# A fused cross-attention and FFN kernel: the next context's parts made earlier, one transpose in another PSUM bank, two copies behind the last exponential

## The reference, cut to what matters

```python
x = x + xattn(layernorm(x), ctx, ctx, wq, wk, wv, wo_w, wo_b)
x = x + ffn(layernorm(x), W_in, b_in, W_out, b_out)
# xattn: q, k rotated (rope), v plain; 16 heads of 32 features; band |q - k| <= 128;
#        softmax(q k^T * sqrt(32)) v, then wo_w and wo_b
# ffn: weights rounded to 8 bits, activations to 16 bits, exact gelu between the products
```

## Time and profile before

| | |
|---|---|
| time before, median of 3 runs | 1230.52 us (1228.41 to 1232.91) |
| profiled execution, its own time | 1230.85 us |
| its span, first to last instruction | 1228.3 us |
| PE busy / DVE busy | 1148.1 us / 979.9 us |
| ACT busy / POOL busy | 639.9 us / 361.2 us |

### The profile page before, as it was taken

How to read it: one execution, slowest core, us unless ns; L and a number is a source line. 1 busy time by engine, 2 the same in 40 slices (tenths; PEclk the granted TensorE clock), 3 DMA queues, 4 the chain that set the end, 5 groups by cost and what they waited for, 6 DMA issues and landing times.

```text
span 1228.3 us, 23590 instructions
## 1 busy us (share of the span) xinstructions
PE 1148.1 (93%) x7884; PEld 767.8 (63%) x7928; DVE 979.9 (80%) x2541; ACT 639.9 (52%) x1001; POOL 361.2 (29%) x540
## 2 busy tenths in 40 slices
PE   6989999999999999999999867999999999999998
PEld 6857776877776777787677545444444444444443
DVE  6868989989899998998998746666666678777776
ACT  5254354345335435434533433655556568777774
POOL 1135336345444534634644331000000012111111
PEclk9989999999999999999999969999999999999999
DMA  8554664565565466456555532455554211667772
GB/s 269 127 135 109 170 175 118 152 176 138 142 177 149 110 173 165 113 164 171 146 139 145 143 121 77 144 204 199 204 206 175 95 60 35 187 219 239 237 223 94
DMA packets 100522, 191.10 MB, mean 156 GB/s; under 512 B 13376, under 2 KB 30912, under 8 KB 100416
## 3 DMA queue, kind: packets, MB, share of 16 engines
q1 hardware_dynamic: 100416, 189.75, 52.4%
HBM read 89.16 MB, written 43.91 MB: 108 GB/s over the span
## 4 chain that ended last, share of the span: by engine, by line
DVE 37%; PE 35%; issue 24%; DMA 2%; ACT 1%; SPq 1%; POOL 0%; DVEq 0%; POOLq 0%
PE bank L858 18%; DVE bank L1192 7%; PE bank L521 4%; PE bank L522 4%; PE bank L523 4%; DVE bn L1138 3%; DVE roped L1218 3%; DVE rt L1215 2%; DVE rt L1216 2%; DVE row_max L1192 2%; PE bank L605 2%; DVE neg_max L1233 2%; DVE x_res L1185 2%; DVE nt_t L292 2%; DVE nt_t L291 1%
## 5 line engine op out<-in xcount | busy, mean ns | idle before, releaser
L1192 DVE CUSTOM_DVE_ANT_0 bank<-bank,mask 128x256 f32<-128x256 f32 x512 | 201.8, 454 | 43.5 <-PE bank L605 36.6
L858 PE MATMUL bank<-wout_int,g_lo 128*128 128x512 bf16 x512 | 193.6, 379 | 1.1
L819 PE MATMUL bank<-qT_lo,win_int 128*128 128x512 bf16 x496 | 188.0, 379 | 1.2
L858 PE MATMUL bank<-wout_int,g_hi 128*128 128x512 bf16 x491 | 185.8, 379 | 0.3 <-issue 0.2
L819 PE MATMUL bank<-qT_hi,win_int 128*128 128x512 bf16 x474 | 179.6, 379 | 0.0
L961 ACT ACTIVATE probs<-bank 128x512 f32<-128x512 f32 x256 | 143.2, 604 | 36.8 <-PE bank L639 32.2
L1529 POOL TENSOR_SCALAR_AFFINE_SELECT probs<-probs 128x256 f32<-128x256 f32 x256 | 108.6, 427 | 80.4 <-ACT probs L961 74.3
L605 PE MATMUL bank<-k_st,q_st 96*128 96x256 f32 x512 | 98.8, 305 | 25.1 <-DVE row_max L1192 23.3
L1484 DVE TENSOR_TENSOR g_lo<-h_int,g_hi 128x512 f16<-128x512 f32 x128 | 89.1, 696 | 41.4 <-ACT g_hi L1101 37.8
L1522 POOL TENSOR_TENSOR x_res<-x_res,wo_b 128x512 f32<-128x512 f32 x32 | 43.4, 1375 | 253.8 <-DMA x_res<-in_x 246.5
L1069 ACT ACTIVATE h_ring<-bank,b_in,g_scale 128x512 f32<-128x512 f32 x96 | 73.0, 778 | 71.3 <-PE bank L819 54.8
(11 more groups left out here) (170 smaller groups left out, 2725.5 us busy)
## 6 DMA issues: line engine op xcount, KB each, us to landing
hidden_scratch<-h_ring SPq DMA_DIRECT2D x96, 256.0 KB, 2.1
h_ring<-hidden_scratch SPq DMA_DIRECT2D x96, 256.0 KB, 2.8
k_st<-k_hi SPq DMA_DIRECT2D x128, 128.0 KB, 2.7
q_st<-q_hi SPq DMA_DIRECT2D x128, 128.0 KB, 2.6
xq<-x_scratch SPq DMA_DIRECT2D x16, 1024.0 KB, 5.9
x_ln<-in_x SPq DMA_DIRECT2D x16, 512.0 KB, 4.5
ctx_raw<-in_ctxT SPq DMA_DIRECT2D x16, 512.0 KB, 5.0
k_st<-k_lo SPq DMA_DIRECT2D x64, 128.0 KB, 2.7
```

Source lines behind the costliest of these rows:

```text
L819: mm = pe.matmul(bank[f % 4][:], win_int[:, c, f * P:(f + 1) * P], part[:, par, c], start=c == 0 and part is qT_hi, stop=c == KC - 1 and p ...
L858: return pe.matmul(bank[4 * par + u][:], part[:, f % 4, u * P:(u + 1) * P], wout_int[:, f], start=f == 0 and part is g_hi, stop=f == FC - ...
L1192: dve.tensor_tensor_reduce(sc, sc, mask[:, (1 - qb) * P:(1 - qb) * P + S], 1.0, NEG, ALU.add, ALU.max, row_max[:, qb, n:n + 1]).then_inc(m ...
```

## The change

Four things move, and nothing is computed differently. (1) Transpose 1 of x goes to bank 6 instead of bank 5. It then waits for `oT_out` (bank 6 copied out in the step before) instead of `den_done`; V tile 0, which writes bank 6 next, waits for `xt_lo`; Q half 1, which writes bank 5, waits for `den_done`. (2) ScalarE's `ctx_hi(b+2)` moves from behind exponential 9 to the front of `max_copy`. (3) GpSimd's four `ctx_lo(b+2)` move from behind bands 10 to 13: two in front of band 0, one behind band 1, one behind band 3. (4) ScalarE's `oT_copy(b, 0)` and `centre(b-1, 0)` move from behind exponentials 12 and 13 to behind the last.

```diff
+        x_bank = [bank[4], bank[6]]
...
                     wait(pe, rope_step["q"], ROPE_OPS * j)
+                elif j == 1:
+                    pe.wait_ge(v_done, 1)
                 else:
-                    wait(pe, den_done, j - 1)
+                    wait(pe, oT_out, 2 * j - 3)
                 for c in range(KC):
-                    mm = pe.transpose(q_bank[s][:, c * P:(c + 1) * P], x_ln[:, s, c * P:(c + 1) * P], ident[:])
+                    mm = pe.transpose(x_bank[s][:, c * P:(c + 1) * P], x_ln[:, s, c * P:(c + 1) * P], ident[:])
... v_tile:
+                if s == 0:
+                    pe.wait_ge(xt_lo, 2 * j + 2)
... qk_tile, "q":
+                else:
+                    wait(pe, den_done, j - 1)
... ScalarE (xt_lead and VectorE's xt_rest read x_bank in place of q_bank):
+                if has_xt:
+                    ctx_hi(b + 2)
                 max_copy(b, 0, slice(0, 2))
                 max_copy(b, 0, slice(2, KC))
                 for n in range(H):
                     softmax_exp(b, n)
                     if n == 6 and has_proj:
                         split_hi("q", b + 1)
-                    if n == 9 and has_xt:
-                        ctx_hi(b + 2)
                     if n in (8, 9, 10, 11) and not has_proj:
                         first_tile(n - 8)
-                    if n == 12:
-                        oT_copy(b, 0)
-                    if n == 13 and has_o:
-                        centre(b - 1, 0)
+                oT_copy(b, 0)
                 if has_o:
+                    centre(b - 1, 0)
                     centre(b - 1, 1)
... GpSimd:
+                if has_xt:
+                    ctx_lo(b + 2, 0)
+                    ctx_lo(b + 2, 1)
                 for n in range(H):
                     band(b, n)
                     if 6 <= n < 10 and has_proj:
                         split_lo("q", b + 1, n - 6)
-                    if 10 <= n < 14 and has_xt:
-                        ctx_lo(b + 2, n - 10)
+                    if n in (1, 3) and has_xt:
+                        ctx_lo(b + 2, n // 2 + 2)
```

More of the change, by code:

```diff
@@ L924, in xt_lead @@
                 act.wait_ge(xt_mm, 2 * j + s + 1)
-                lead(q_bank, s, xt_hi)
+                lead(x_bank, s, xt_hi)
             def oT_copy(j, half):
@@ L1228, in xt_rest @@
             def xt_rest(j, s):
-                rest(q_bank, s, xt_hi, 2 * j + s + 1, xt_lo)
+                rest(x_bank, s, xt_hi, 2 * j + s + 1, xt_lo)
             def invert(b):
```

## The result

The changed kernel took 1246.13 us (median of 4 runs, 1245.47 to 1248.04). The ratio to the kernel before is 1.0126, with a 95% interval from 1.0104 to 1.0149. I had forecast 1219 us; it became 1.3% slower. The profiled execution took 1246.22 us.

The account below looks back on a forecast made before the run. Neither PE nor VectorE alone bounds the kernel; they hand work to each other. Per step 1.52 us usable gain minus 0.7 lost is 0.82, times 14 plus 0.4: 11.9 off 1230.85, so 1219 us, range 1208 to 1230.

Parts of the forecast that it names:

- Both waits: PE's waits forecast to go: 0.51 us for `invert` before transpose 1, 1.10 us for the last band before clump 3.
- the mechanism that the earlier trace show: At the step's end, small `ln1` instructions on VectorE end with the GpSimd instruction beside them; fewer `ctx_lo` gain 1.4 us.
- V tile 0 did not wait: Sign of being wrong: V tile 0 waiting for `xt_rest`, with 1.08 us margin before; costed at nothing.
- the 0.7 us that I took as lost in the second half: Moved `ctx_lo` at the second half's start: 0.4 us at L1199, 0.3 us for late `split_lo` of Q; bounds 0 to 2.5.
- the sum: Per step: 1.8 us earlier, 1.52 usable within the reciprocals' slack, 0.7 lost, so 0.82 us net gain.
- One sign that I had named for being wrong: The first `split_lo` of Q coming more than 1 us late after the maxima.
- the 13 slacks: Slack of the reciprocals' DMA before `normalise` in steps 2 to 14: 0.2 to 3.4 us, mean 1.87.
- The port's cost at `neg_max`: L1199 on VectorE waiting for the first moved `ctx_lo` on GpSimd, ahead of `max_transposes`: 0.4 us lost per step.
- The 0.70 us of the bank: Transpose 1 in bank 6 no longer waits for `invert`, making PE 0.70 us earlier per step.
- C: Rival, chance 0.11: slower by the port, L1199, L1218 and `split_lo` of Q delayed 2.5 us per step; 1241 us.
- A: Rival, chance 0.16: the port costs little and the DMA loop gives way; 1208 us.
- B: Rival, chance 0.15: the reciprocals' DMA loop takes all the gain, `normalise` waiting in every step; 1230 us.

Follow-up runs that it names:

- e5: Changed kernel plus one GpSimd wait, so the first `ctx_lo` starts only after VectorE's two `neg_max` instructions; 1225.16 us, 0.9952 of the kernel before.
- e2: Kernel before with all of the change except transpose 1 of x in bank 6 and its waits; 1247.71 us, ratio 1.0143.
- e3: Changed kernel plus 12 small unused matmuls on PE before the scores of head 14; 1238.97 us, 1.0071 of the kernel before.
- e9: Changed kernel plus unused matmuls on PE, 10 before the scores of head 14 and 8 before `max_transposes`; 1233.79 us, 1.0028 of the kernel before.
- e12: e8 plus 5 small unused matmuls on PE before the scores of head 14; 1213.35 us, 0.9862 of the kernel before.
- e6: Kernel before with the reciprocals' store issued ahead of `load_xres`, nothing of the change; 1229.23 us, ratio 0.9982.
- e10: Kernel before with only `oT_copy(b, 0)` and `centre(b-1, 0)` moved behind the last exponential; 1230.58 us, ratio 1.0003.
- e8: Changed kernel with the first `ctx_lo` waiting for `neg_max` and the reciprocals stored ahead of `load_xres`; 1217.82 us, 0.9902 of the kernel before.

## Why the prediction was wrong

**What held.** Both waits went away. `ln1` got shorter, by the mechanism that the earlier trace rows show. Three of the last instructions of `ln1` in step 12, which ran at full clock:

```profile
621.41 0.26 DVE L293 SCALAR_TENSOR_TENSOR nt_t<-nt_t,veps 128x2 f32<-128x2 f32 x1
621.71 0.16 DVE L294 SCALAR_TENSOR_TENSOR rstd<-nt_t,rstd 128x2 f32<-128x2 f32 x1
621.90 0.26 DVE L1156 SCALAR_TENSOR_TENSOR nmr<-mv,rstd 128x2 f32<-128x2 f32 x1
```

It ends at 622.16, 0.30 us ahead of that step's `w_transposes` (622.46); before it ended 1.86 us behind them (389.49 against 387.63). That is 2.2 us gained where I took 1.4 and bounded at 2.0, and PE reaches the end of V tile 1 2.0 us earlier where I took 1.8. V tile 0 did not wait. Of the 0.7 us that I took as lost in the second half, the 0.3 us for a late `split_lo` of Q measured nothing at full clock (7.04 us behind `max_transposes`, before and after).

**What failed.** The step that failed is the sum, in what it took for granted: that a microsecond in which PE waits costs that microsecond and no more. I had read PE's idle time as waits to be removed, and did not ask where it would be gathered. PE came 2.1 us earlier to the end of V tile 1 (means of steps 2 to 14), but VectorE's `normalise` started only 1.3 us earlier and ended only 1.0 us earlier, and so PE's wait for heads 13 to 15 grew from 0.3 us in most steps to as much as 2.7. Behind it the granted clock fell in 11 of 14 steps. The forecast doesn't speak of the clock at all, though the page from which the earlier trace rows come has a row for it, and none of the rivals had a price for it.

In its place the runs show this account of a step: 2.0 us gained up to V tile 1, 1.9 us lost from there to `max_transposes`, 1.4 us lost behind it, which makes 1.3 us longer and not 0.82 shorter. The 1.4 us is the half clock alone. Of the 1.9 us at most 0.5 is the half clock (14.9 us in 14 steps, of which half is lost if PE has work throughout); the rest, 1.4 or more, is waiting. So I estimate the step without the half clock, with the same waits, at 43.2 to 43.7 us; step 12, at full clock, took 43.63. The clock thus turned a small gain (0.1 to 0.6 us per step) into a loss of 1.3%, but the 43.0 that I had forecast would have been missed without it too.

One sign that I had named for being wrong did show: the first `split_lo` of Q came 1.2 to 2.5 us later behind `max_transposes` in 11 of 14 steps. I had meant it as a sign that GpSimd is late, and it was the clock.

**What was mis-sized.** The wait of `normalise` for the reciprocals: 7.1 us in 9 of 13 steps, where the 13 slacks and 1.8 us gave 3.6 us. `normalise` itself: 1.99 us against 1.62 before (the same means), which I had put at nothing. The port's cost at `neg_max`: 0.4 us forecast, 1.05 measured by the medians (L1202 0.77 against 0.18, L1204 0.66 against 0.19). I had let only L1199 (now L1204) wait, since its neighbour L1197 (now L1202) ran at 0.18 us beside the end of `ot_rest`. Both wait, each for one `ctx_lo`. The trace of before could have told me, in `ln1`, where an instruction of the same operation as L1202 starts beside a `ctx_lo` (384.46 to 385.19) and ends with it:

```profile
384.46 0.73 POOL L1512 TENSOR_TENSOR cT_lo<-ctx_raw,cT_hi 128x256 fp32r<-128x256 f32 x1
...
384.55 0.68 DVE L286 TENSOR_SCALAR rstd<-rstd 128x2 int32<-128x2 int32 x1
```

The Trainium skill (SBUF — State Buffer, "Who interferes with whom") names `tensor_scalar` among the operations that can take the shared pair; the trace agrees for L1202 (0.77 against 0.18 us), and I had weighed the rule for L1199 alone. By itself the second wait would have cost 0.65 us more per step; e5, which removes both, gained 0.83 us per step in front of `max_transposes` and another 0.82 behind it, where the clock fell less. The 0.70 us of the bank was counted on top of a gain that contained it (e2), and the larger gain of `ln1` hid that: that PE came about as early as forecast is in part luck.

**The rivals.** C named the side on which it came out, but not its mechanism: it made `split_lo` of Q late by GpSimd's and L1218's waits, and at full clock these cost nothing. Its 1241 is near by accident. A and B are out by their times.

**What stays open.** The same wait did not bring the same clock each time: in step 12 of the changed kernel PE waited 1.71 us before head 14 and kept its full clock, while 0.67 us in step 10 brought 3.4 us of half clock. Both steps had 0.8 us before `max_transposes`. Which idle time brings the fall these runs don't settle. Steps with half clock also differ in their waits, so the link from the gathered waits to the fall rests on the fillers (e3, e9, e12) and on e5. And e9 stays above e3's best execution by 0.5 us per step in front of `max_transposes`, which I can't put down to one cause.

## What to carry to other kernels

When a change lets PE run ahead of the engine it depends on, write down where the removed idle time will be gathered, and look at the granted clock of that stretch, not only at the sum of the waits. Here PE, at 93% busy, lost more with its idle time in one place, up to 2.7 and 1.5 us, than with the same idle time in pieces of 0.3 to 1.1. If the gap can't be closed, a few matmuls about as long as it are worth a try (e12, and only in part e3 and e9); and before moving work to an idle engine, list the small instructions of the other engine that it will stand beside.

## What the runs showed of the hardware

- The same work, from `max_transposes` to the first `split_lo` of Q, took 7.04 us at the full clock and 8.28 to 9.59 us in steps that met 3.4 or 6.8 us of half clock: 19.4 us lost for 43.1 us of half clock.
- Idle time of nearly the same sum (35.8 and 35.1 us from 120 to 700 us) went with no half clock when it lay in three places of the step (3.4 us in e6 and in e10, which place it alike), and with 58 us of it when it lay in one.
- Work that isn't needed can pay: 12 unused matmuls per step took 7 us off the changed kernel, 5 per step took 4.5 us off e8 (1217.82 to 1213.35).
- One wait added on GpSimd took 21 us off the program (e5 against the change); the first `split_lo` of Q came no later for it (7.03 to 7.05 us behind `max_transposes` in e5's steps at full clock).
- VectorE's `tensor_scalar` from float32 to fp32r on 128x32 elements takes 0.18 us alone and 0.77 us when a GpSimd `tensor_tensor` stands in its way (medians of L1197 before and L1202 after).
